# Linear attention moved into the layers' block, with two banks for its last products, and the stage ahead of a convolution in another order

## The reference

```
h = layernorm(x) * (1 + ca) + sa
x = x + ga * linear_attention(h)            # 2 heads of 64, gated, RMS norm, output weights
h = layernorm(x) * (1 + cb) + sb
x = x + gb * two_layers(h)                  # each: windowed attention (8 heads of 64, window 64,
                                            # rotary embedding), then a gated MLP with GELU
h = layernorm(x) * (1 + ca') + sa'
z = softmax over the positions of h @ W_A.T * 8 ** -0.5   # 16 heads
x = x + ga' * (causal convolution of z with h @ W_V.T) @ W_O.T + ...
h = layernorm(x) * (1 + cb') + sb'
x = x + gb' * top2_of_16_experts(h)
```

## Time and profile before

| | us |
|---|---|
| median of 3 runs (1161.91 to 1164.67) | 1164.17 |
| the profiled execution, its own time | 1171.24 |
| its span, first to last instruction | 1169.4 |
| PE busy | 1058.9 (91%) |
| DVE busy | 898.9 (77%) |
| ACT busy | 850.3 (73%) |
| GpSimd busy | 659.6 (56%) |

### The profile page before, as it was taken

How to read it: one execution, slowest core, us unless ns; L and a number is a source line. 1 busy time by engine, 2 the same in 40 slices (tenths; PEclk the granted TensorE clock), 3 DMA queues, 4 the chain that set the end, 5 groups by cost and what they waited for, 6 DMA issues and landing times. The chain is left out here.

```text
span 1169.4 us, 33840 instructions
## 1 busy us (share of the span) xinstructions
PE 1058.9 (91%) x11683; PEld 728.6 (62%) x11683; DVE 898.9 (77%) x2972; ACT 850.3 (73%) x2674; POOL 659.6 (56%) x1070
## 2 busy tenths in 40 slices
PE   5799997489999999899799999998899799999996
PEld 3576765157777776556477777776566498853442
DVE  4679999478888888665688888888586555289998
ACT  3578886388988898633588888988444766378886
POOL 1468997588888888510588888888233400002222
PEclk9589999699999999999899999999999899999998
DMA  7000000021222212141112122121101342100000
GB/s 238 4 1 5 18 3 2 0 52 46 60 55 55 47 42 47 44 133 35 40 38 49 45 47 47 39 47 42 27 1 38 81 125 77 34 8 14 19 17 18
DMA packets 66498, 50.86 MB, mean 43 GB/s; under 512 B 42262, under 2 KB 53442, under 8 KB 66050
## 3 DMA queue, kind: packets, MB, share of 16 engines
q1 hardware_dynamic: 66339, 48.84, 16.4%
HBM read 21.41 MB, written 2.38 MB: 20 GB/s over the span
## 5 line engine op out<-in xcount | busy, mean ns | idle before, releaser
L1168 PE MATMUL psum<-wa_wqkv,wa_hT 128*128 128x512 f32 x384 | 189.9, 603 | 4.3 <-DVE wa_tmp L1032 3.1
L1124 ACT ACTIVATE wa_p<-psum,wa_nb 128x128 f32<-128x128 f32 x512 | 183.8, 398 | 2.1 <-DVE wa_nb L1048 1.9
L1048 DVE CUSTOM_DVE_ANT_0 psum<-psum,wa_bias 128x128 f32<-128x128 f32 x512 | 132.9, 322 | 50.3 <-PE psum L1197 50.3
L1014 POOL TENSOR_TENSOR wa_p<-wa_p,wa_rrs 128x512 f32<-128x512 f32 x128 | 133.1, 1040 | 43.7 <-DVE wa_rrs L1057 43.7
L1711 POOL TENSOR_TENSOR ex_total<-ex_total,mod 128x128 f32<-128x128 f32 x32 | 15.5, 484 | 214.6 <-DVE ex_total L1839 214.6
L1124 ACT ACTIVATION_READ_ACCUMULATOR wa_p<-psum,wa_nb 128x1 f32 x512 | 122.4, 239 | 0.0
L985 POOL TENSOR_TENSOR wa_qr<-wa_qr,wa_tmp 128x512 f32<-128x512 f32 x64 | 81.7, 1277 | 71.5 <-DVE wa_tmp L1032 71.5
L1886 ACT ACTIVATE cv_z_ex_yw<-psum,ex_w 128x128 f32<-128x128 f32 x384 | 106.7, 400 | 20.2 <-DVE ex_w L1815 7.4
L1957 PE MATMUL psum<-ex_wc,ex_hT 128*128 128x512 f32 x256 | 117.4, 603 | 3.7 <-DVE cv_z_ex_yw L1822 2.7
L1134 ACT ACTIVATE wa_pT<-psum 128x512 f32<-128x512 f32 x128 | 76.6, 598 | 37.7 <-PE psum L1177 37.7
L1177 PE MATMUL psum<-ident,wa_p 128*128 128x128 f32 x512 | 79.7, 278 | 9.6 <-ACT wa_kT L1117 2.9
(11 more groups left out here) (258 smaller groups left out, 3003.1 us busy)
## 6 DMA issues: line engine op xcount, KB each, us to landing
wa_vm<-wa_v SPq DMA_DIRECT2D x127, 128.0 KB, 2.3
cv_toep<-cv_zpad SPq DMA_DIRECT2D x32, 136.0 KB, 2.7
cv_toep<-cv_zpad SPq DMA_DIRECT2D x16, 264.0 KB, 4.1
wa_tabs<-in_rotations_dram SPq DMA_DIRECT2D x2, 2048.0 KB, 8.1
wa_rows<-y_rows SPq DMA_DIRECT2D x31, 128.0 KB
wa_rows<-y_rows SPq DMA_DIRECT2D x31, 127.0 KB
x_rows<-in_L_attn_x_dram SPq DMA_DIRECT2D x4, 512.0 KB, 6.2
out_dram<-x_rows SPq DMA_DIRECT2D x32, 64.0 KB, 1.5
```

The costliest lines, as they stand in the source:

```text
L1014: nc.gpsimd.tensor_tensor(p, p, cols_bc(rrs[:, t % 2, r, :], P), ALU.mult)\
L1048: m = nc.vector.tensor_tensor_reduce(out=s, in0=s, in1=edges, scale=-1.0, scalar=MAX_FLOAT, op0=ALU.add, op1=ALU.min, accum_out=nb[:, t % ...
L1124: e = nc.scalar.activation(pr[:, t % 2, r, h, :], sim_bank[r][:, P * h:P * h + P], ACT.Exp, bias=nb[:, t % 2, r, h:h + 1], scale=-1.0, acc ...
L1168: nc.tensor.matmul(bank, hT[:, t % 3, :], wqkv[:, INNER * k:INNER * k + INNER], start=True, stop=True).then_inc(done.sem, 1)
```

## The change

3. From tile 29 on the output products take two banks in turn:

```
+    TWO_BANKS = TILES - 3
+    o_product = lambda t: out if t >= TWO_BANKS and (t - TWO_BANKS) % 2 == 0 else wide
...
         def o_project(t):
             v_og.wait(pe, t)
-            take("wide", v_res[1], t)
-            nc.tensor.matmul(wide[:, 0:GH * E], ogT[:, t % 6, :],
+            if t == TWO_BANKS:
+                v_og.wait(pe, TILES - 1)
+            else:
+                v_res[1].wait(pe, t - 1 if t < TWO_BANKS else t - 2)
+            nc.tensor.matmul(o_product(t)[:, 0:GH * E], ogT[:, t % 6, :],
```

4. The four table scalings on DVE move from L36 to the start of L5, L6, L7 and L8, one in each:

```
-                between[36] = lambda: prepare_next.vector(dve)
+        for k in range(4):
+            between[5 + k] = lambda k=k: given.vector(dve, k)
```

6. All banks of the layers are renamed, and layer 0's first use of each bank now waits for its last reader in linear attention:

```
-    BANKS = ((0, 1, 2, 3, 4, 5, 6, 7), (0, 1, 2, 6, 7, 5, 4, 3))
+    BANKS = ((2, 3, 5, 0, 4, 6, 1, 7), (2, 3, 5, 1, 7, 6, 4, 0))
...
-    BANKS = ((0, 1, 2), (5, 4, 7), 6, 3), ((0, 1, 2), (5, 7, 3), 4, 6)
+    BANKS = ((2, 3, 5), (6, 4, 7), 1, 0), ((2, 3, 5), (6, 7, 0), 4, 1)
...
+    left = {0: (v_q, last), 1: (a_rr, last), 2: (a_s, last), 3: (v_prod, last), 4: (v_base, last), 5: (v_base, last),
+            6: (v_res[1], last), 7: (v_res[1], last)}
```

7. Ahead of the convolution, GpSimd and DVE alternate between the groups, and the small things on DVE and the two softmaxes stand elsewhere:

```
 # GpSimd
-                for g in late:
-                    conv.gated(gp, g)
-                for g in late:
-                    conv.inverse_std(gp, g)
+                for g in range(conv.IN_MLP, GROUPS + 1):
+                    if g < GROUPS:
+                        conv.gated(gp, g)
+                    if g > conv.IN_MLP:
+                        conv.inverse_std(gp, g - 1)
 # DVE
-                for g in late:
-                    conv.statistics(dve, g)
-                for g in late:
-                    conv.offsets(dve, g)
-                weights()
-                on_vector.mixing(dve)
+                for g in range(conv.IN_MLP, GROUPS + 1):
+                    if g < GROUPS:
+                        conv.statistics(dve, g)
+                    if g > conv.IN_MLP:
+                        conv.offsets(dve, g - 1)
                 for g in range(GROUPS):
                     group_max(g)
                     if g == PER_B - 1:
+                        weights()
+                        on_vector.mixing(dve)
+                    if g == PER_B + 1:
                         probabilities(0)
-                probabilities(1)
...
                 on_vector.add_bias(dve, 0)
+                probabilities(1)
 # ACT
-                    if g == PER_B + 1:
+                    if g == PER_B + 2:
                         z_exp(0)
-                z_exp(1)
...
                 for r in range(1, len(PARTS)):
                     lower_rows(0, r)
+                z_exp(1)
```

More of the change, by code:

```diff
@@ L164, with __init__ @@
 class Phase:
-    def __init__(self, stages, first, n, between=None, begin=None):
+    def __init__(self, stages, first, n, between=None, begin=None, longer=None, more=0):
         self.stages, self.first, self.n = stages, first, n
         self.between, self.begin = between or {}, begin
+        self.longer, self.more = longer, more
     def step(self, s):
@@ L175, in step @@
         for f, lag in self.stages:
-            if 0 <= s - lag < self.n:
+            if 0 <= s - lag < self.n + (self.more if f is self.longer else 0):
                 f(self.first + s - lag)
@@ L226, in linear_attention @@
[L226 to L247, removed]
@@ new lines, in linear_attention, with in_turn @@
+    sem = lambda name: c.sem(ctx, "la_" + name)
+    signal = lambda name, every=1: Signal(sem(name), every=every)
+    def in_turn(name, n, every=1):
+        s = sem(name)
+        return [Signal(s, k, n, every) for k in range(n)]
+    c_in, w_in = sem("c_in"), sem("w_in")
+    x_in = [sem(f"x_in{k}") for k in range(TILES // CHUNK)]
+    g_set, v_set, a_set, p_set = sem("g_set"), sem("v_set"), sem("a_set"), sem("p_set")
+    v_xst, v_xb = in_turn("v_xst_xb", 2, CHUNK)
+    a_lx, a_xs = in_turn("a_log_xs", 2, CHUNK)
@@ L758, in row_statistics @@
+    last = TILES - 1
+    left = {0: (v_q, last), 1: (a_rr, last), 2: (a_s, last), 3: (v_prod, last), 4: (v_base, last), 5: (v_base, last),
+            6: (v_res[1], last), 7: (v_res[1], last)}
+    return (sync, gpsimd, vector, scalar, tensor), left
 def row_statistics(c, ctx, tag):
@@ L842, in first_loads, with stage_normalized @@
         self.load_layer(sp, 0)
+        self.y_done = y_done
         for i, n in self.PORTIONS[:self.AHEAD]:
-            y_done.wait(sp, i + n - 1)
-            self.stage(sp, "attention", 0, i, n)
+            self.stage_normalized(sp, i, n)
+    def stage_normalized(self, sp, i, n):
+        self.y_done.wait(sp, i + n - 1)
+        self.stage(sp, "attention", 0, i, n)
     def gpsimd(self, gp):
@@ L1018, in gpsimd @@
             return Phase([(scale_q, 2), (scale_k, 2), (scale_p(0), 3), (add_q, 1), (clip, 1),
-                          (scale_p(1), 3), (add_k, 1)], first, TILES, begin=None if l else lambda: at_start(gp))
+                          (scale_p(1), 3), (add_k, 1)], first, TILES,
+                         between=None if l else {s: lambda f=f: f(gp) for s, f in between.items()})
         def vector(dve):
@@ L1077, in vector @@
                           (rotate_q, 1), (norms, 1), (reciprocal(1), 3), (rotate_k, 1), (residual, 5)], first, TILES,
-                         begin=tables_ready)
+                         between={1: tables_ready})
         def scalar(act):
```

950 lines of the change are left out of this document (476 added, 474 removed).

## The result

The changed kernel takes **1154.66 us** (median of 4 runs, 1152.14 to 1155.75), the kernel before 1164.42 in the same comparison: 9.8 us less, or 0.9916 of it. The ratio recorded for this comparison is 0.9903, with a 95% interval of 0.9876 to 0.9929, which isn't exactly that of the medians and would be 11.3 us. Measured once more on another occasion it gave 0.9877 (0.9856 to 0.9897). The forecast was 14.45 less, the range 1143 to 1158 us. The profiled execution of the changed kernel is itself one of 1154.24 us (span 1152.5), while the one of before was 7 us above its median. So I compare stretches between two events inside the traces, not times from the start.

The account below looks back on a forecast made before the run. What counts is where PE lacks work: the join between linear attention and layers, and ahead of the convolution. -12.4 + 1.15 + 0.4 - 3.6 = -14.45 gives 1156.8 profiled, 1149.7 (say 1150) after the step to the median; range 1143 to 1158 us.

Parts of the forecast that it names:

- Join, -12.4: Linear attention into the layers: scores of the fourth windowed step start at 222.0 instead of 234.4; ends -11.4 and -13.7.
- the rival in which the join brings less: Stretched linear tail: longer DVE waits for PE and ACT, or late keys from GpSimd; fourth step at 226, 1154 us; chance 0.2.
- A0, "+0.3": First windowed step, woven into linear attention's tail: priced as one transpose on PE, +0.3 us.
- The chain behind it: Linear tail after the first woven step: second step's projections and rotations, masked copy, last gated product, third step, residuals.
- The hold-up of the masked copy: Last linear tile's copy on DVE waits behind the second windowed step's rotations: 197.15 becomes 204.4, a new wait of 7.25 us.
- Ramp, +1.15: Fourth to ninth windowed steps, with the last linear attention work beside them: +1.15 us; ends 0 and +4.1.
- Scalings, +0.4: Four table scalings of 1.29 us moved to the start of linear steps L5 to L8: +0.4; ends 0 and +5.1.
- the cover named: Early linear attention: PE at half clock hides the moved scalings; at full clock all 5.1 us would be on the path.
- Convolution, -3.6: Ahead of the convolution: start 4.9 us earlier (4.1 plus 0.8), second round 1.3 late; bounds -5.5 and -1.
- The loads of Toeplitz rows: Ahead of the convolution: issued later, taken as hidden; the rival has them bound, 1152.3 us, chance 0.15.
- the chain from A2 to A3: Third to fourth windowed step: four times statistics and residual at 1.16, a shift 0.16, waits 0.6; from 215.1 or 217.4 to 220.7 or 223.0.
- the last rival: Whole change: nothing measurable, with full scaling price, +4.1 in the ramp and -1 at the convolution; -3.3, 1161 us; chance 0.02.

Follow-up runs that it names:

- the late softmax: Changed kernel with the second softmax moved behind the copies for the convolution's third round instead of the first: 1152.05 us, ratio 0.9870 to the kernel before.
- the unwoven kernel: Changed kernel with no merged steps, windowed attention beginning only after linear attention's last step: 1151.76 us, ratio 0.9881 to the kernel before.
- the last kernel of the table: Changed kernel with first two windowed steps behind L34 and L35, next four behind L40 to L43, second softmax later: 1141.78 us, ratio 0.9809 to the kernel before.

## Why the prediction was right, and where it was not

The range held, and the time came out 4.7 above the forecast of 1150 in the first measurement, and at it, by the ratio, in the second. The terms, by the traces:

- **Join, -12.4: it is -7.7 to -9.2.** From L31 to A3 it took 52.6 and takes 43.4, and 44.7 to 45.0 in four other traces with the same join. That A3 began at 221.90, as forecast (222.0), is luck: L31 itself was 3.3 earlier, because the low clock at the start of that execution ended at 56.5 and not at 69.6 (in the two other traces in which it ended at 69.6 and 69.8, L31 is at 181.9 and 182.2). Counted from L31 as it was before, A3 stands at 225 to 227: the rival in which the join brings less, with its 226 and 1154 us, came true in its size, but not by the waits that it names.
- **The step that failed is A0, "+0.3".** I priced its transpose on PE and forgot its copy on ACT, which stands ahead of L33's decays. L34's last product came 19.5 after L31 in place of 15.5: 4.0 and not 0.3 (3.7 to 4.0 in all six traces with A0 there). The wait is the smaller part of it: in the three traces in which the clock was still full, L33's last product came 1.3 late (13.0 after L31 for 11.7). The rest falls into the 6.8 to 10.2 us at 0.50 that follow in all six; none of the eight other traces is at 0.50 before L34's last product. Put behind L34, A0 leaves L34's last product at 15.5, and the next one comes 0.3 late, as I had it.
- **The chain behind it held.** From L34's last product (197.95) to the masked copy 6.4 us (7.8 to 8.0 in the five other traces; forecast 7.1), from its end to that of the last gated product 3.1 (2.3 to 3.0), A2 6.7 us, half of it at the low clock (7.0), the residuals 1.2 apart. The hold-up of the masked copy was real (10.5 to 11.9 late after L31, with A0's part in it; I had 7), and could be avoided.
- **Ramp, +1.15: it is +1.8**, A3 to A8 took 41.1 for 39.4. A3 to A4 took 9.3, in a stretch at 0.50 until 227.1.
- **Scalings, +0.4: 0.3**, by the step from L8 to L9 (5.5, 5.2 before). But the cover named was not what hid them: PE at half clock was there only for the first two in this execution, and in another, with full clock from 45.3, four of them cost 1.1 together. At L20 to L23 they cost 3.1, not 5.1. What the steps L5 to L8 have and the later ones lack is room on DVE, which does its first residual (lag 9) at 73.2 only: from 58.04 to 67.41, at full clock, it is busy 8.77 of 9.37 with two scalings of 1.3 in it, so some 6.2 without them, where later it has 57.30 of 60.00.
- **Convolution, -3.6: -3.8.** The start came 5.5 nearer and not 4.9; the second round was 1.3 late, as worked out, and the late softmax shows the cause, but another 0.4 went in the next rounds. ACT went on 2.7 earlier after the block's start (forecast 3.0), with 0.63 of waiting (0.4). The loads of Toeplitz rows stayed hidden: PE waits for ACT's copy of v.

Up to A8 it is -7.4 or -6.3 (92.0 against 84.6 and 85.7); with +0.3 and -3.8 that makes -10.9 or -9.8, where the two timings say -9.8 and -15.3 by the medians, -11.3 and -14.3 by the ratios (of 1164.42). My sum had join and ramp 4 to 5 too good. That the range held owes something to its width. Two slips of adding stand in the prediction: the chain from A2 to A3 adds up to 0.2 less than it says, and the last rival's terms to -4.2 (1160), not -3.3 (1161).

What the forecast had wrong in kind: it followed one chain through the new timetable, as if the weaving made the gain. The block of scalings in the tail, one bank, and the wait for GpSimd's last row made up 12.2, and taking them away needs no weaving; the weaving as it was placed gave 3.0 to 4.6 of that back at A3, and 1.7 in the ramp, by the traces; in the timings the woven and the unwoven kernel can't be told apart.

## What to carry to other kernels

When one edit removes a barrier, moves work out of the way and interleaves two phases, price each of the three alone, and ask first what the join would be without the interleaving. A step put into another phase's tail costs what stands behind it on every queue, its smallest copy too: put it behind the last thing that the tail's chain needs from that engine, here two steps later for A0 and one for A1. And compare stretches between two events of a trace, since the start of the trace may differ by chance.

## What the runs showed of the hardware

- One kernel's executions differ, and with them the mean granted clock: 41 of the kernel before took 1161.0 to 1171.2 us at mean clocks of 0.977 to 0.962. Over the 117 executions of all 13 kernels with a clock on record, lines of one slope, with a level for each kernel, fit with 0.59 us less for each 0.001 of clock more, and leave 1.0 us. At a clock of 0.976 they give 1162.8 before, 1153.9 changed, 1153.6 unwoven and 1147.1 for the last kernel of the table.
- At the start the low clock ended anywhere between 44.7 and 69.8 us, with nearly the same instructions on PE up to there. Tables of stretches, first of the changed kernel's second trace, then of before:

```profile
46.00:57.00 11.00, 9.28 (x119) 6.83 (x119) 10.40 (x24) 8.24 (x19) 8.58 (x25) 1.00 0.01 3
```

```profile
44.00:57.00 13.00, 12.22 (x108) 9.56 (x109) 7.78 (x20) 7.10 (x17) 7.30 (x28) 0.50 0.01 3
```

- DVE's first addition ahead of the convolution starts when GpSimd has done its first product. It took 1.75 where GpSimd had one more product to do and 2.98 where it had two more; both times it ended 0.6 after GpSimd had stopped. All 14 traces have one of these two lengths within 0.01, by the order of the kernel. The Trainium skill (SBUF — State Buffer, Who interferes with whom) says that a DVE instruction with two SBUF inputs contends with a GpSimd instruction that reads SBUF; these traces agree, 1.75 and 2.98 against 0.68, and here the length follows how long GpSimd goes on.
